# Softmax denominators as two products of 64 columns over 512 instead of four of 32 over 256

## The chip, the core and the metric

The kernel runs on one core of a Trainium2 chip. The metric is the device time of one execution in microseconds (us). The core has TensorE (PE in the profile; PEld is its weight load), VectorE (DVE), ScalarE (ACT), GpSimd (POOL), and a queue, SP, that issues all transfers.

## The reference

One transformer block in float32 on x of shape (2, 2048, 256): layer norm without weights, attention with 16 heads of 64 and a causal mask, an output projection, a residual sum, then layer norm, one linear layer (its weight is W plus a low-rank product) and a second residual sum.

```
qkv = layernorm(x) @ W_qkv                    # 256 -> 3 * 16 * 64
score = einsum('bihd,bjhd->bijh', q, k) / 8   # causal mask
wmat = softmax(score, axis=2)                 # over the keys j
x = x + einsum('bijh,bjhd->bihd', wmat, v).reshape(b, l, 1024) @ W_out
x = x + layernorm(x) @ (W + lilora_weight).T + b
```

The change is in the softmax: the sum over the keys, by which the product of the exponentials with v is divided.

## The kernel before

The program has three blocks, one behind the other: projection of q, k and v (`project_qkv`), attention (`attention`), and output projection with the linear layer (`project_and_ffn`). q, k, v and the attention's output `o_t` lie in DRAM between them.

Attention works on 16 items: 8 pairs of heads times 2 batches. The two heads of a pair share the 128 partitions, 64 each. An item has 4 tiles of 512 queries, t = 0 to 3. A unit (t, j) is 128 keys against the 512 queries of tile t, for both heads; tile t has 4(t + 1) units, so that an item has 40. All engines run an order written out by hand, over pairs of units:

- PE makes the scores of two units ahead (`score_unit`: float32r products of 64 rows and 128 columns, and small bf16 ones), chunks for the next item in between (`chunk_products`, L863: scores with queries as rows, of which DVE takes the row maxima), then the products with v for the two units (`pv_unit`, L899). The last are float32: weights of 128x64 for each head, the two heads side by side, over 512 columns of the exponentials. A float32 product shows as two matmul records, one for each of its two passes.
- ACT makes the exponentials (L964), copies the finished output of a tile out of PSUM (`copy_o`, L973), and at the start of an item also casts the next q and k.
- The exponentials `probs` are summed over the units, element by element: POOL adds the full units into `sum_pool` (L1147), DVE adds those on the diagonal and then `sum_pool` into `sum_dve` (L1059 to L1079). DVE also reduces the chunks to `part_max` (L1033).
- PSUM has a ring of three banks. A chunk takes two of them, a denominator one, in turn. PE waits before it reuses one, on DVE's reductions or on ACT's copy of the denominators (`ring_free`).

The denominators of tile t still need the sum of `sum_dve` over the 128 partitions. `denominators` makes it as a product with ones, which gives the sums to all rows of the output. It is queued on PE after the first pair of units of the next tile (for t = 3, of the next item). Then:

1. ACT copies the bank to `den_row` (L993), behind the exponential of the fourth unit of that tile.
2. SP sends one row of each product to `den_spread` (L742, `invert`), 4 values to a partition.
3. DVE takes the reciprocal (L1099), in its fixed order behind work of the sixth unit, so DVE stands still if the transfer has not landed.
4. SP stores it to `r_t` (L746), and loads it back with each head's row spread over 64 partitions (`recip`, two issues, L750).
5. POOL multiplies (`normalise`, `o_norm`, L1132), and SP stores the tile (L735).

SP runs all this in one order for an item: the last tile of the item before, then t = 0; the first half of a coming item's k and q (two loads of 512 KB, `load_piece`), t = 1; the second half, t = 2; at the end it places the row maxima of the next item in `shift` (`place_max`, four issues, L771). The first scores of the next item wait for these. Each `invert` comes behind the store of the tile before. The last item has no chunks. In it SP loads parts of `o_t` for the next block in these places.

The last denominators of all (item 15, t = 3) are made in the next block, in a bank of `y`, after the first tile of the output projection (L1368, L1407, `finish_last_o`).

Of the kernel before, what the change touches and what calls it, by code (L numbers as in the profile page):

```python
# [18 lines left out]
P = 128  # L19
# [8 lines left out]
TILE = 512  # L28
NB = TILE // P
EPS = 1e-5  # L30
STAGES = 3
DEN = TILE // 2
LOADS = 2
PARTS = 4
LOWEST = -3.0e38
# [27 lines left out]
def wait_apart(eng, sem, value, other, least):  # L63


    value = value if isinstance(value, int) else eng.to_reg(value)
    eng.wait_ge(other, least)
    eng.wait_ge(sem, value)
# [472 lines left out]
def attention(nc, q_t, k_t, v, o_t, r_t, w_out, batches, scale, consts, lead, tail):  # L541
# [5 lines left out]
    D = hd // HEADS  # L547
    assert 2 * D == P and batches == 2
    PAIRS = HEADS // 2
    TI = L // TILE  # L550
# [45 lines left out]
    ring_banks, at = {}, 0  # L596
# [58 lines left out]
    head = lambda h: slice(h * D, (h + 1) * D)  # L655
# [4 lines left out]
    with ctx:  # L660
        sb = lambda name, shape, dt=F32: ctx.enter_context(nc.sbuf_tensor("b_" + name, shape, dt))
# [11 lines left out]
        o_raw, o_norm, recip, sum_dve = tail["o_raw"], tail["o_norm"], tail["recip"], tail["sum_dve"]  # L673
        den_row, den_spread, recip_spread = tail["den_row"], tail["den_spread"], tail["recip_spread"]
# [8 lines left out]
        ring = ps("ring", [P, RING, TILE])  # L683
# [15 lines left out]
        den_copied, den_moved, inverted = tail["den_copied"], tail["den_moved"], tail["inverted"]  # L699
# [15 lines left out]
        with nc.Block() as block:  # L715

            @block.sync
            def _(sp):
# [18 lines left out]
                def invert(n, t):  # L737

                    wait_apart(sp, den_copied, n * TI + t + 2, o_stored, 1)
                    for c in range(4):  # L740
                        h, half = divmod(c, 2)
                        sp.dma_start(den_spread[half * D:(half + 1) * D, h, :], den_row[c * P // 4:c * P // 4 + 1, :].rearrange(  # L742
                            "o (p i) -> o p i", i=NB)).then_inc(den_moved, 16)

                    wait_apart(sp, inverted, n * TI + t + 1, o_stored, 1)
                    sp.dma_start(r_t[t].rearrange("h (p i) -> p h i", i=NB), recip_spread[:]).then_inc(inverse_stored, 16)  # L746

                    wait_apart(sp, inverse_stored, (n * TI + t + 1) * 16, o_stored, 1)
                    for h in range(2):
                        sp.dma_start(recip[h * D:(h + 1) * D, :], r_t[t, h:h + 1, :].broadcast_to([D, TILE])  # L750
                                     ).then_inc(recip_loaded, 16)
# [62 lines left out]
            def _(pe):  # L814
# [88 lines left out]
                def denominators(n, t, now, before):  # L903

                    pe.wait_ge(dve_added, sum_ready[n, t])
                    ring_free(now, before)
                    denom = ring[:, ring_banks["denom", t][0], :]
                    for c in range(4):
                        h, half = divmod(c, 2)
                        cols = slice(half * DEN, (half + 1) * DEN)  # L910
                        last = nc.tensor.matmul(denom[c * P // 4:(c + 1) * P // 4, 0:DEN], consts["ones"][:, 0:P // 4],
                                                sum_dve[t % 2][:, h, cols], start=True, stop=True)
                    last.then_inc(denom_made, 1)

                def item(pair, u, following, previous=True):
# [28 lines left out]
            def _(act):  # L944
# [43 lines left out]
                def copy_denominators(n, t):  # L988

                    act.wait_ge(denom_made, n * TI + t + 1)  # L990
                    act.wait_ge(den_moved, (n * TI + t) * 64 + 1)
                    denom = ring[:, ring_banks["denom", t][0], 0:DEN]
                    nc.scalar.copy(den_row[:], denom).then_inc(den_copied, 1)  # L993

                def item(pair, u, following, previous=True):
# [30 lines left out]
            def _(dve):  # L1026
# [68 lines left out]

                def reciprocals(n, t):

                    dve.wait_ge(den_moved, (n * TI + t + 1) * 64 + 1)
                    nc.vector.reciprocal(recip_spread[:], den_spread[:]).then_inc(inverted, 1)  # L1099

                def item(pair, u, following, previous=True):
# [59 lines left out]
def project_and_ffn(nc, x, o_t, r_t, bias, ffn_weights, out, consts, tail):  # L1161
# [10 lines left out]
    with ctx:  # L1172
        sb = lambda name, shape, dt=F32: ctx.enter_context(nc.sbuf_tensor("c_" + name, shape, dt))
# [27 lines left out]
        y = [ctx.enter_context(nc.psum_tensor(f"c_y{u}", [P, NB, cin], F32)) for u in range(2)]  # L1201
# [30 lines left out]
        all_pairs = HEADS // 2  # L1232
        o_tiles = tiles * all_pairs
        last_t = tiles // 2 - 1
        last_denom = y[1][:, 0, 0:DEN]

        with nc.Block() as block:

            @block.sync
            def _(sp):  # L1240
# [29 lines left out]
                def finish_last_o():  # L1270

                    sp.wait_ge(tail["den_copied"], o_tiles + 1)
                    for c in range(4):
                        h, half = divmod(c, 2)
                        sp.dma_start(tail["den_spread"][half * P // 2:(half + 1) * P // 2, h, :],
                                     tail["den_row"][c * P // 4:c * P // 4 + 1, :].rearrange("o (p i) -> o p i", i=NB)
                                     ).then_inc(tail["den_moved"], 16)

                    sp.wait_ge(tail["inverted"], o_tiles)
                    sp.dma_start(r_t[last_t].rearrange("h (p i) -> p h i", i=NB), tail["recip_spread"][:]  # L1280
                                 ).then_inc(tail["inverse_stored"], 16)

                    sp.wait_ge(tail["inverse_stored"], o_tiles * 16)
                    for h in range(2):
                        sp.dma_start(tail["recip"][h * P // 2:(h + 1) * P // 2, :],
                                     r_t[last_t, h:h + 1, :].broadcast_to([P // 2, TILE])).then_inc(tail["recip_loaded"], 16)

                    sp.wait_ge(tail["o_ready"], o_tiles + 2)
                    sp.dma_start(o_t[hd - P:hd, tokens - TILE:tokens], tail["o_norm"][:]).then_inc(tail["o_stored"], 16)
# [26 lines left out]
            def _(pe):  # L1316
# [45 lines left out]
                out_project(0, 0, [0, 1, 2, 3])  # L1362

                pe.wait_ge(tail["dve_added"], tail["dve_ops"])
                for c in range(4):
                    h, half = divmod(c, 2)
                    cols = slice(half * DEN, (half + 1) * DEN)
                    last = nc.tensor.matmul(last_denom[c * P // 4:(c + 1) * P // 4, :], consts["ones"][:, 0:P // 4],  # L1368
                                            tail["sum_dve"][last_t % 2][:, h, cols], start=True, stop=True)
                last.then_inc(tail["denom_made"], 1)  # L1370
                pe.wait_ge(merge_loaded, 16 * 5)
                nc.tensor.matmul(d_ps, down[:], aux[:], start=True, stop=True).then_inc(d_made, 1)
# [3 lines left out]
                for c in range(C):  # L1376
                    last = nc.tensor.matmul(l_ps[:, c, :], t_sb[:, c * P:(c + 1) * P], up_aux[:], start=True, stop=True)
# [7 lines left out]
            @block.scalar  # L1385
            def _(act):
                def high(T, u, loads):

                    act.wait_ge(o_loaded[u], (loads - (u == 0)) * 16)
                    act.wait_ge(y_made, T + 1)  # L1390
                    nc.scalar.copy(o_hi[u][:], o_in[u][:]).then_inc(o_hi_ready, 1)

                def take_root(T, u):

                    act.wait_ge(var_ready, T + 1)
                    nc.scalar.activation(root[u][:], var_eps[u][:], ACT.Sqrt).then_inc(root_ready, 1)  # L1396

                def turn(T, u):

                    act.wait_ge(transposed, T + 1)  # L1400
                    nc.scalar.copy(xt[u][:], turned[:]).then_inc(xt_ready, 1)

                act.sem_inc(y_made, 2)
                high(1, 1, 1)
                act.wait_ge(tail["denom_made"], o_tiles)
                act.wait_ge(tail["den_moved"], (o_tiles - 1) * 64 + 1)
                nc.scalar.copy(tail["den_row"][:], last_denom).then_inc(tail["den_copied"], 1)  # L1407
                take_root(0, 0)
                for i in range(halfway - 1):
                    turn(i * 2, 0)  # L1410
                    high(i * 2 + 2, 0, i + 2)
                    take_root(i * 2 + 1, 1)
                    turn(i * 2 + 1, 1)
                    high(i * 2 + 3, 1, i + 2)
                    take_root(i * 2 + 2, 0)
                turn(tiles - 2, 0)
                take_root(tiles - 1, 1)
                turn(tiles - 1, 1)

            @block.vector  # L1420
            def _(dve):
# [51 lines left out]
                dve.wait_ge(merge_loaded, 16 * 5)  # L1473
                nc.vector.tensor_tensor(w_ffn_t[:], l_ps, w_in[:], ALU.add).then_inc(merged, 1)
                norm(0, 0, 1)
                dve.wait_ge(tail["den_moved"], o_tiles * 64 + 1)
                nc.vector.reciprocal(tail["recip_spread"][:], tail["den_spread"][:]).then_inc(tail["inverted"], 1)
                for i in range(halfway - 1):
                    low(i * 2 + 2, 0)
# [31 lines left out]
def attend(nc, rows, w_qkv, w_out, bias, ffn_weights, out_rows, drams, batches, length, scale, consts):  # L1511
    q_t, k_t, v, o_t, r_t = drams
    with ExitStack() as ctx:
        sb = lambda name, shape, dt=F32: ctx.enter_context(nc.sbuf_tensor("f_" + name, shape, dt))
# [19 lines left out]
        with ExitStack() as later:  # L1534
            sb = lambda name, shape, dt=F32: later.enter_context(nc.sbuf_tensor("g_" + name, shape, dt))
# [5 lines left out]
                "o_norm": sb("o_norm", [P, TILE]),  # L1541
                "sum_dve": [sb(f"sum_dve{i}", [P, 2, TILE]) for i in range(2)],
                "recip": sb("recip", [P, TILE]),
                "den_row": sb("den_row", [P, DEN]),
                "den_spread": sb("den_spread", [P, 2, NB]),
                "recip_spread": sb("recip_spread", [P, 2, NB]),
                "o_in": [lead["raw"][:].rearrange("p a b (c t) -> p (a b c) t", t=TILE), sb("o_in1", [P, KC, TILE])],
# [69 lines left out]
```

## Time and profile before

| | |
|---|---|
| median of 3 runs | 1877.65 us (1874.08 to 1879.98) |
| the profiled execution | 1877.58 us, span 1875.8 us |
| mean granted clock of TensorE | 0.992 |
| PE, DVE, POOL, ACT busy | 95%, 66%, 52%, 42% |
| attention block | from about 330 to 1725 us of the span |

The span runs from the first to the last instruction of the core; the device time has 1.8 us around it. An idle time is put down to what ended it. Matmuls are pipelined, so that starts are firmer than ends.

### The profile page before, as it was taken

Reading aid. Unit: us, or ns where it says so; the run is one execution under the profiler, and the core shown is the slowest. Engines: PE = TensorE matmul, PEld = TensorE weight load, DVE = VectorE, ACT = ScalarE, POOL = GpSimd, SP = SyncE. Lnnn points to the kernel's source line nnn. Section 1 sums busy time; section 2 is a strip of 40 time slices with the busy share of each in tenths; the row PEclk is TensorE's granted clock in tenths of the full one; section 3 lists DMA queues with packets and bytes.
Section 4 is the critical chain, followed back from the end, with each engine's and each line's share of the span. In section 5 each row is a group of like instructions: output and inputs, shape, how many; then the busy total and the mean of one; then the engine's idle time right before and its main releaser. Section 6 shows DMA issues by size and latency. Waiting matters only on the chain. (4 is left out here: it accounts for less than half of the span.)

```text
span 1875.8 us, 34882 instructions
## 1 busy us (share of the span) xinstructions
PE 1780.3 (95%) x13720; PEld 1055.6 (56%) x13720; DVE 1246.0 (66%) x2091; ACT 789.0 (42%) x982; POOL 968.6 (52%) x532
## 2 busy tenths in 40 slices
PE   7999998999999999999999999999999999998998
PEld 5877776545545444445445455454554455444897
DVE  5364652767676767676767767676767677747565
ACT  3222113454545454545354454545454545454221
POOL 1011000666675758485766656676657585746211
PEclk9999999999999999999999999999999999999999
DMA  5646445212121212122121223121212121023551
GB/s 207 225 180 233 165 157 210 73 47 80 42 74 47 69 52 69 47 69 75 46 69 47 81 57 80 35 80 41 74 47 71 50 69 52 24 75 115 183 181 57
DMA packets 153858, 171.39 MB, mean 91 GB/s; under 512 B 48202, under 2 KB 94816, under 8 KB 153696
## 3 DMA queue, kind: packets, MB, share of 16 engines
q1 hardware_dynamic: 153696, 169.17, 28.7%
q8 instruction: 110, 1.80, 0.4%
q14 instruction: 52, 0.43, 0.1%
HBM read 97.02 MB, written 71.57 MB: 90 GB/s over the span
## 5 line engine op out<-in xcount | busy, mean ns | idle before, releaser
L1033 DVE TENSOR_REDUCE f_part_max<-b_ring 128x1 f32<-128x512 f32 (+3 forms) x1200 | 675.4, 604 | 290.5 <-PE b_ring L863 193.4
L964 ACT ACTIVATE b_probs<-b_scores 128x1024 f32<-128x1024 f32 (+3 forms) x640 | 564.6, 898 | 608.2 <-PE b_scores L834 342.7
L1147 POOL TENSOR_TENSOR b_sum_pool<-b_sum_pool,b_probs 128x1024 f32<-128x1024 f32 x237 | 569.4, 2403 | 32.1 <-POOL b_sum_pool L1147 0.5
L834 PE MATMUL b_scores<-b_split 64*128 64x512 f32 (+2 forms) x1920 | 296.8, 418 | 0.0
L834 PE MATMUL b_scores<-f_split 64*128 64x512 f32 (+2 forms) x1920 | 296.1, 416 | 0.0
L1147 POOL TENSOR_TENSOR b_sum_pool<-b_probs 128x1024 f32<-128x1024 f32 x48 | 114.7, 2389 | 309.8 <-DVE g_sum_dve L1079 198.1
L899 PE MATMUL b_o_acc<-b_probs,b_v_in 128*64 128x512 f32 (+3 forms) x1280 | 269.5, 542 | 2.3 <-ACT b_probs L964 2.3
L899 PE MATMUL b_o_acc<-b_probs,f_v_in 128*64 128x512 f32 (+3 forms) x1280 | 270.4, 543 | 0.0
L834 PEld LDWEIGHTS b_scores<-b_split 64*128 64x128 f32 x1920 | 179.8, 189 | 12.2
L834 PEld LDWEIGHTS b_scores<-f_split 64*128 64x128 f32 x1920 | 179.9, 188 | 11.0
L1073 DVE TENSOR_TENSOR g_sum_dve<-g_sum_dve,b_probs 128x768 f32<-128x768 f32 (+2 forms) x195 | 160.3, 822 | 35.5 <-ACT b_probs L964 30.9
L863 PE MATMUL b_ring<-b_split 64*128 64x512 f32 (+2 forms) x640 | 143.0, 434 | 18.3 <-DVE f_part_max L1033 17.3
L348 DVE COPY a_stage_d<-a_made 128x512 f32<-128x512 f32 x96 | 66.2, 691 | 140.8 <-PE a_made L293 140.7
L348 ACT COPY a_stage_a<-a_made 128x512 f32<-128x512 f32 x96 | 56.5, 589 | 224.7 <-PE a_made L293 223.4
L863 PE MATMUL b_ring<-f_split 64*128 64x512 f32 (+2 forms) x560 | 125.4, 436 | 17.4 <-DVE f_part_max L1033 16.3
L899 PEld LDWEIGHTS b_o_acc<-b_probs,b_v_in 128*64 128x64 f32 x1280 | 77.8, 136 | 112.2 <-issue 81.4
L899 PEld LDWEIGHTS b_o_acc<-b_probs,f_v_in 128*64 128x64 f32 x1280 | 77.9, 136 | 108.7 <-issue 80.9
L863 PEld LDWEIGHTS b_ring<-b_split 64*128 64x128 f32 x640 | 64.7, 183 | 128.6 <-issue 124.2
L830 PE MATMUL b_scores<-f_shift,p_first_rows 64*128 64x512 bf16 (+2 forms) x640 | 117.6, 356 | 14.8 <-ACT b_probs L964 10.5
L830 PE MATMUL b_scores<-b_shift,p_first_rows 64*128 64x512 bf16 (+2 forms) x640 | 118.2, 359 | 9.0 <-issue 4.6
L863 PEld LDWEIGHTS b_ring<-f_split 64*128 64x128 f32 x560 | 56.6, 184 | 114.6 <-issue 110.4
L712 POOL TENSOR_TENSOR b_split<-f_raw,b_split 128x512 fp32r<-128x512 f32 x64 | 81.5, 1297 | 59.6 <-ACT b_split L950 59.6
(138 smaller groups left out, 2219.2 us busy)
## 6 DMA issues: line engine op xcount, KB each, us to landing
f_raw<-k_t SPq DMA_DIRECT2D x32, 512.0 KB, 4.7
f_raw<-q_t SPq DMA_DIRECT2D x32, 512.0 KB, 5.8
g_recip<-r_t SPq DMA_DIRECT2D x128, 128.0 KB, 3.0
o_t<-g_o_norm SPq DMA_DIRECT2D x64, 256.0 KB, 2.0
q_t<-a_stage_a SPq DMA_DIRECT2D x32, 256.0 KB, 2.3
q_t<-a_stage_d SPq DMA_DIRECT2D x32, 256.0 KB, 2.0
k_t<-a_stage_a SPq DMA_DIRECT2D x32, 256.0 KB, 2.0
k_t<-a_stage_d SPq DMA_DIRECT2D x32, 256.0 KB, 2.0
```

The costliest lines, as they stand in the source:

```text
L348: copy(stage[e][s][:], made[:, g % BANKS, :]).then_inc(emptied[e], 1)
L712: vec.tensor_tensor(lo[u][:, cols], raw[p][:, which, inner], halves(hi[u][:, cols]), ALU.subtract).then_inc(split_lo, 1)
L830: nc.tensor.matmul(scores[s % 2][:, h, lo:TILE], consts["first_rows"][head(h), :], shift[u][head(h), queries], start=True, stop=False)
L834: last = nc.tensor.matmul(scores[s % 2][:, h, lo:TILE], a[u][head(h), keys], b[u][head(h), queries], start=False, stop=(term == 2 and not ...
L863: last = nc.tensor.matmul(rowwise[h][:, 0:wide], q_hi[u][head(h), ib * P:(ib + 1) * P], k_hi[u][head(h), c * TILE:c * TILE + wide], start= ...
L899: last = nc.tensor.matmul(o_acc[head(h), off:], v_in[u][:, j, head(h)], probs[s % PR][:, h, off:], start=(j == 0), stop=(j == NB * t + NB ...
L964: nc.scalar.activation(probs[s % PR][:, :, off:], scores[s % 2][:, :, off:], ACT.Exp, scale=scale).then_inc(exp_done, 1)
L1033: nc.vector.tensor_reduce(part_max[:, h, ib, c:c + 1], rowwise[h][:, 0:width], AX.X, ALU.max).then_inc(chunk_reduced, 1)
L1073: nc.vector.tensor_tensor(sum_dve[t % 2][:, :, off:], sum_dve[t % 2][:, :, off:], probs[s % PR][:, :, off:], ALU.add).then_inc(dve_added, 1)
L1147: nc.gpsimd.tensor_tensor(sum_pool[:], first, probs[s % PR][:], ALU.add).then_inc(pool_added, 1)
```

## The change

The product with ones had four parts: head h and half of the queries, weights of 128x32, 256 columns, each to its own 32 rows of the bank. Now it has two, one for each head: weights of 128x64, 512 columns, each to its own 64 rows. The bank's row 0 then has all 512 denominators of the first head and row 64 those of the second. So ACT's copy takes 512 columns instead of 256, `den_row` doubles, and SP sends two rows of 512 values (128 pieces of 16 bytes) instead of four of 256 (64 pieces each). The waits on `den_moved` count 32 for a tile instead of 64. The last denominators, in the third block, change in the same way, and their part of `y` is two sub-tiles wide instead of one.

```diff
 def invert(n, t):
-    for c in range(4):
-        h, half = divmod(c, 2)
-        sp.dma_start(den_spread[half * D:(half + 1) * D, h, :], den_row[c * P // 4:c * P // 4 + 1, :].rearrange(
+    for h in range(2):
+        sp.dma_start(den_spread[:, h, :], den_row[h * D:h * D + 1, :].rearrange(
             "o (p i) -> o p i", i=NB)).then_inc(den_moved, 16)
 def denominators(n, t, now, before):
-    for c in range(4):
-        h, half = divmod(c, 2)
-        cols = slice(half * DEN, (half + 1) * DEN)
-        last = nc.tensor.matmul(denom[c * P // 4:(c + 1) * P // 4, 0:DEN], consts["ones"][:, 0:P // 4],
-                                sum_dve[t % 2][:, h, cols], start=True, stop=True)
+    for h in range(2):
+        last = nc.tensor.matmul(denom[head(h), :], consts["ones"][:, 0:D],
+                                sum_dve[t % 2][:, h, :], start=True, stop=True)
 def copy_denominators(n, t):
-    act.wait_ge(den_moved, (n * TI + t) * 64 + 1)
-    denom = ring[:, ring_banks["denom", t][0], 0:DEN]
+    act.wait_ge(den_moved, (n * TI + t) * 32 + 1)
+    denom = ring[:, ring_banks["denom", t][0], :]
     nc.scalar.copy(den_row[:], denom).then_inc(den_copied, 1)
 def reciprocals(n, t):
-    dve.wait_ge(den_moved, (n * TI + t + 1) * 64 + 1)
+    dve.wait_ge(den_moved, (n * TI + t + 1) * 32 + 1)
...
-                "den_row": sb("den_row", [P, DEN]),
+                "den_row": sb("den_row", [P, TILE]),
```

## Rows read from the trace of the kernel before

**Rows 1.** The page's busy times: us, share of the span, instructions.

```profile
PE 1780.3 (95%) x13720; PEld 1055.6 (56%) x13720; DVE 1246.0 (66%) x2091; ACT 789.0 (42%) x982; POOL 968.6 (52%) x532
```

**Rows 2.** Windows: length, busy PE, PEld, DVE, ACT, POOL, granted clock, DMA share, GB/s.

```profile
412.60:1647.70 1235.10, 1186.61 (x10096) 617.25 (x10094) 886.75 (x1486) 588.81 (x727) 814.12 (x419) 1.00 0.22 60
...
412.67:500.10 87.43, 84.80 (x723) 43.95 (x721) 63.30 (x107) 42.17 (x53) 57.62 (x30) 1.00 0.22 62
```

**Rows 3.** Waits from 412 to 1640 us: who for whom, us in total, times, longest.

```profile
PE b_ring L863 <- DVE f_part_max L1033: 32.5, 49, 1.8
...
DVE g_recip_spread L1099 <- DMA g_den_spread<-g_den_row: 19.3, 26, 2.0
...
PE b_scores L830 <- issue: 6.5, 13, 1.5
```

**Rows 4.** Timeline of PE, item 1 (start us, us); middle two rows from narrower windows.

```profile
436.63 1.94 PE L899 MATMUL b_o_acc<-b_probs,b_v_in 128*64 128x512 f32 x8
438.50 0.64 PE L911 MATMUL b_ring<-g_sum_dve,p_ones 128*32 128x256 f32 x8
439.07 0.50 PE L863 MATMUL b_ring<-f_split 64*128 64x512 f32 x2
...
437.11 1.03 PE L899 MATMUL b_o_acc<-b_probs,b_v_in 128*64 128x512 f32 x4
...
437.54 1.03 PE L899 MATMUL b_o_acc<-b_probs,b_v_in 128*64 128x512 f32 x4
...
442.24 1.94 PE L899 MATMUL b_o_acc<-b_probs,b_v_in 128*64 128x512 f32 x8
444.11 0.50 PE L863 MATMUL b_ring<-f_split 64*128 64x512 f32 x2
```

**Rows 5.** ACT: copies by source line (ns min/median/max), and its timeline after one.

```profile
L993 ACT COPY g_den_row<-b_ring x63: 372/373/375, 334.6 to 1695.9; 128x256 f32<-128x256 f32 x63
...
L973 ACT COPY g_o_raw<-b_o_acc x64: 582/587/602, 329.8 to 1720.9; 128x512 f32<-128x512 f32 x64
...
422.63 1.96 ACT L964 ACTIVATE b_probs<-b_scores 128x1024 f32<-128x1024 f32 x2 [1.03 <-PE b_scores L842]
```

**Rows 6.** SP: issues by source line (ns), and a row of its timeline.

```profile
L742 SPq DMA_DIRECT2D g_den_spread<-g_den_row x252: 474/589/1832, 335.0 to 1698.2; - x126
...
L746 SPq DMA_DIRECT2D r_t<-g_recip_spread x63: 365/376/379, 344.2 to 1704.5; - x63
...
427.74 2.40 SPq L742 DMA_DIRECT2D g_den_spread<-g_den_row  x4
```

**Rows 7.** Timeline of DVE: reciprocals at t = 0 (three items) and t = 1.

```profile
431.38 0.20 DVE L1099 RECIPROCAL g_recip_spread<-g_den_spread 128x8 f32<-128x8 f32 x1 [0.29 <-DMA g_den_spread<-g_den_row]
...
785.72 0.20 DVE L1099 RECIPROCAL g_recip_spread<-g_den_spread 128x8 f32<-128x8 f32 x1 [1.97 <-DMA g_den_spread<-g_den_row]
...
1579.23 0.20 DVE L1099 RECIPROCAL g_recip_spread<-g_den_spread 128x8 f32<-128x8 f32 x1 [0.28 <-DMA g_den_spread<-g_den_row]
...
449.26 0.20 DVE L1099 RECIPROCAL g_recip_spread<-g_den_spread 128x8 f32<-128x8 f32 x1 [0.83 <-DMA g_den_spread<-g_den_row]
```

**Rows 8.** Timeline of PE: the last chunk of t = 0 in items 0 and 1.

```profile
348.83 0.50 PE L863 MATMUL b_ring<-b_split 64*128 64x512 f32 x2 [0.35 <-DVE f_part_max L1033]
...
436.21 0.49 PE L863 MATMUL b_ring<-f_split 64*128 64x512 f32 x2 [0.65 <-DVE f_part_max L1033]
```

**Rows 9.** Timelines of POOL, SP and PE up to the start of item 2.

```profile
465.96 22.53 POOL L1147 TENSOR_TENSOR b_sum_pool<-b_sum_pool,b_probs 128x1024 f32<-128x1024 f32 x9
...
492.07 0.59 SPq L771 DMA_DIRECT2D f_shift<-f_max_low  x1
...
493.89 0.39 PE L830 MATMUL b_scores<-f_shift,p_first_rows 64*128 64x512 bf16 x2 [0.22 <-issue]
```

**Rows 10.** Timelines of PE and DVE in the last item.

```profile
1671.34 1.08 PE L911 MATMUL b_ring<-g_sum_dve,p_ones 128*32 128x256 f32 x8 [2.28 <-DVE g_sum_dve L1079]
...
1682.68 0.20 DVE L1099 RECIPROCAL g_recip_spread<-g_den_spread 128x8 f32<-128x8 f32 x1 [11.39 <-DMA g_den_spread<-g_den_row]
```

More of the change, by code:

```diff
@@ L31 @@
 STAGES = 3
-DEN = TILE // 2
 LOADS = 2
@@ L1234, in project_and_ffn @@
         last_t = tiles // 2 - 1
-        last_denom = y[1][:, 0, 0:DEN]
+        last_denom = y[1][:, 0:2, :].rearrange("p n c -> p (n c)")
         with nc.Block() as block:
@@ L1272, in finish_last_o @@
                     sp.wait_ge(tail["den_copied"], o_tiles + 1)
[L1273 to L1277, printed above, removed]
+                    for h in range(2):
+                        sp.dma_start(tail["den_spread"][:, h, :], tail["den_row"][h * P // 2:h * P // 2 + 1, :].rearrange(
+                            "o (p i) -> o p i", i=NB)).then_inc(tail["den_moved"], 16)
                     sp.wait_ge(tail["inverted"], o_tiles)
@@ L1364, in _ @@
                 pe.wait_ge(tail["dve_added"], tail["dve_ops"])
[L1365 to L1369, printed above, removed]
+                for h in range(2):
+                    half = slice(h * P // 2, (h + 1) * P // 2)
+                    last = nc.tensor.matmul(last_denom[half, :], consts["ones"][:, 0:P // 2],
+                                            tail["sum_dve"][last_t % 2][:, h, :], start=True, stop=True)
                 last.then_inc(tail["denom_made"], 1)
@@ L1405, in _ @@
                 act.wait_ge(tail["denom_made"], o_tiles)
-                act.wait_ge(tail["den_moved"], (o_tiles - 1) * 64 + 1)
+                act.wait_ge(tail["den_moved"], (o_tiles - 1) * 32 + 1)
                 nc.scalar.copy(tail["den_row"][:], last_denom).then_inc(tail["den_copied"], 1)
@@ L1475, in _ @@
                 norm(0, 0, 1)
-                dve.wait_ge(tail["den_moved"], o_tiles * 64 + 1)
+                dve.wait_ge(tail["den_moved"], o_tiles * 32 + 1)
                 nc.vector.reciprocal(tail["recip_spread"][:], tail["den_spread"][:]).then_inc(tail["inverted"], 1)
```

## The prediction

> **What bounds the kernel now.** I read the page first [rows 1]: PE is busy 95% of the span, the next engine, DVE, 66%, and the clock is granted nearly throughout. Busy time alone proves little for pipelined matmuls, so I looked at the stretches next [rows 2]. The even part of the attention block, 412.6 to 1647.7 us, is 66% of the span, has PE busy for 1186.6 of its 1235.1 us (96%), and runs at the full clock (1.00, which is 2.4 GHz). The waits of PE in it [rows 3] are short: 32.5 us in 49 waits for `part_max` reductions on DVE and 6.5 us in 13 waits at the start of an item; those left are smaller. Together that is 3% of 1228 us. So a PE cost inside the block reaches the end of the kernel unless a wait that something else sets lies behind it. I therefore price the change on PE first, and then ask, for each of the four places where denominators are made in an item, whether the next wait is set by PE itself or by a chain that does not notice PE.
>
> **The product on PE.** The denominators run side by side in four column groups. They show as eight matmul records, two passes of four, and hold PE from 438.50 to 439.07, 0.57 us [rows 4]; the other products with a chunk behind them look the same. The new form is not in the trace, but its shape is: the product with V is two side-by-side 128x64 products over 512 columns in the same type. Eight of its records (two units, four passes) take 436.63 to 438.50, 1.87 us. Inside, a pass follows its like after 0.43 (437.11 to 437.54), the first pass takes 0.48, which leaves 1.87 - 0.48 - 2 x 0.43 = 0.53 for the last, whether a 128x32 product follows (438.50) or a 64x128 one (442.24 to 444.11, also 1.87). So I read 0.10 as the price of a change of shape. Before, there is such a change on both sides of the denominators. After, they have V's shape, and the one ahead goes. The step from the last pass of V to the next chunk is 0.53 + 0.57 = 1.10 before, and 0.43 + 0.43 + 0.53 = 1.39 after: **+0.29 us** each. From below, nothing cheaper than V's own passes is to be expected, since the columns that stream double; if the 0.10 ahead stayed it would be +0.39, and if the first pass were V's 0.48 too, +0.44. I take 0.29, because the last V pass costs the same whatever waits stand in front of the instruction behind it.
>
> The Trainium skill, TensorEngine Tiling (Array Packing), section Key Properties, says that changing the tiling mode drains the engine, while another tile of the same mode does not; by that rule the increment is 0.29, without it 0.39. The same page's section When to Use Tiling gives 64 columns a factor of two where 32 have four, which speaks against the change; the records of V and of the denominators agree.
>
> **ACT.** The copy of 256 columns takes 0.373, one of 512 columns from PSUM 0.587 [rows 5]: +0.21 us, 64 times. After the copy ACT idles 1.03 us for scores [rows 5], which PE makes later by the same amount as it ends the product, so the copy hides with 0.8 to spare. At t = 3 (15 times) ACT has casts of the next item around it and that idle time isn't there; PE is two units of scores behind ACT then, and I take it as hidden too. Without that cover its price would be 0.21 x 15 = 3 us.
>
> **The DMA chain.** SP issues four pieces in 2.40 us, 0.6 each (427.74 to 430.14), and the reciprocal starts at 431.38 [rows 6, 7]. A store of 256 pieces of 16 bytes takes SP 0.37 [rows 6], so an issue doesn't grow with its pieces in this range; two issues save 2 x 0.62 = **1.24 us** of the chain. The bounds are 0 (an issue of 128 pieces costs twice one of 64) and 1.24.
>
> **Which place is worth what.** Item n holds tiles t = 0 to 3; the product for a tile comes after the first V pair of the next.
> - t = 3 (15 times): nothing external follows soon. +0.29 each, **+4.4**.
> - t = 0 (n = 0 to 14 here, 15 times): +0.29 each, +4.4. In items 1 to 14 SP can send these denominators only after it has issued the store of the previous tile's `o_norm`, and DVE stands idle at the reciprocal for them: 0.29 in the first of the 14, 1.97 in the worst, 0.28 in the last, 8.8 in sum [rows 7]. Behind the reciprocal on DVE are the reductions that free the ring for PE. PE waits 0.65 for them at 436.21, but only 0.35 at 348.83 in item 0, where the reciprocal had no wait [rows 8]; the 0.30 is the missing 0.29. So this idle passes to PE one for one. With 1.24 less chain and 0.29 more PE time ahead, all goes but 0.4 of the worst: **-8.4**.
> - t = 1 (15 times): +0.29 each, **+4.4**. DVE idles at this reciprocal too (0.83 at 449.26), behind two 512 KB loads that SP issues just ahead [rows 7], so earlier issues hardly move the landing. PE makes the chunks around it without a wait, since two of the ring's three banks are ahead of DVE there. No gain is booked.
> - t = 2 (15 times): absorbed. POOL adds for t = 3 without a gap, nine adds from 465.96 in 22.53 us, then makes `o_norm`; SP stores it, and only then issues the four pieces that place the next maxima, the last at 492.07. PE's first score of the next item waits for these, until 493.89 [rows 9]. Thirteen such waits are listed, 6.5 us, 0.5 on average, 0.22 in the case shown, from a modelled end of the matmul before [rows 3, 9]. The chain starts before the product of t = 2 and hears nothing of it, so a PE that comes 0.29 later waits 0.29 less: **0**. The shortest waits may leave 0.07 each, 1 us in all; uncovered it would be +4.4.
> - The last item (no chunks): PE waits 2.28 for DVE at 1671.34, which comes out of a wait for `den_spread`, and DVE waits 11.39 for the next one [rows 10]. The three products of this item are absorbed. These two landings are behind 512 KB loads again, so out of 2 x 1.24 I book half, **-1.2**.
> - Tail: one product more on PE in the first output tile, **+0.3**.
>
> Sum: 13.1 - 8.4 - 1.2 + 0.3 = **+3.8 us**. The profiled execution took 1877.58, span 1875.8 and 1.8 around it, and the median of the runs is 1877.65, so both give 1881.4; I say **1881**. That is 0.2%, and a measurement of this kernel can tell 0.3% (5.6 us) from no change.
>
> **Rivals.**
> 1. The change of shape costs nothing, and the 0.10 stays ahead of the product: 45 x 0.39 = 17.6, and 15 x 0.05 more where the item's start absorbs only about 0.34. 17.6 + 0.8 - 9.6 + 0.3 = +9, 1887. For it: before, a product of V never has another tile's product of its own shape behind it, only its own next unit. Against: the even 0.53.
> 2. The DMA relief does not come, as 128 pieces cost twice an issue or land later. Then at t = 0 DVE's idle only shrinks by the 0.29 that PE is late, 4.1 in 14: 13.1 - 4.1 + 0.3 = +9, 1887. Against it is the 0.37 row.
> 3. Nothing absorbs, PE alone sets the time: 64 x 0.29 = +19, 1896. Against it are the waits of rows 7 to 9.
> 4. Faster: the reciprocal's idle passes to PE at t = 1 as well. Its 26 waits between 412 and 1640 sum to 19.3 [rows 3], of which t = 0 holds 8.8; if all went, 13.1 + 0.3 - 19.3 - 1.2 = -7, 1870.5. It falls below the 0.3% from about 17.8 us of them. Against it are the loads ahead.
>
> Single issues of `den_spread` took up to 1.83 us where the median is 0.59 [rows 6]. Which items these hit will differ from run to run, 1.2 us each, and I allow plus or minus 3 us for it in any case.
>
> **The numbers.** Forecast 0.60 (its own range 1877 to 1886), rivals 1 and 2 0.13 and 0.12, rival 3 0.07, rival 4 0.08. Below -0.3%: 0.08. Beyond +0.3%: rival 3, nearly all of 1 and 2 (0.22), and 0.12 of the forecast, 0.41. The rest, 0.51, is within. The range reaches to rivals 1 and 2 with 3 us behind them, and halfway to rival 4: 1873 to 1890.
>
> **What would show it.** Right: half as many records of the product (four for each) in about 0.96 us to the next chunk, and a last V pass of 0.43 ahead of them; copy 0.59; two issues in 1.2; hardly any idle at the t = 0 reciprocals, PE's wait in that place near 0.35, and the start-of-item waits 0.3 shorter. Wrong: a product of 1.05 or more, `den_spread` landing as late as before, or items that grow by 1.2 us each (no absorption). An item here goes 87.43 us in its undisturbed form [rows 2]; I expect 88.0.

## The result

The changed kernel takes 1881.27 us (median of 9 runs, 1878.58 to 1885.05), the kernel before on the same chips 1876.92 (9 runs, 1872.52 to 1882.61): a ratio of 1.0028, 95% interval 1.0015 to 1.0042. It is slower by 5.3 us, give or take 2.5; the forecast was 3.8. The ratios given here and below are estimates over all runs with their intervals, so they differ a little from the quotient of the two medians (here 1.0023).

The page of the changed kernel, its busy times [as rows 1]:

```profile
PE 1796.2 (96%) x13464; PEld 1063.3 (57%) x13464; DVE 1234.1 (66%) x2091; ACT 803.7 (43%) x982; POOL 962.6 (51%) x532
```

PE has 256 records fewer (64 products by 4) and is busy 16 us longer. Windows, as in rows 2: the same stretch, and item 1.

```profile
412.60:1647.70 1235.10, 1200.05 (x9876) 624.92 (x9874) 880.40 (x1487) 602.89 (x729) 807.22 (x419) 1.00 0.21 60
413.46:501.26 87.80, 85.84 (x708) 44.52 (x706) 62.56 (x107) 43.14 (x53) 57.66 (x30) 1.00 0.22 62
```

Waits from 412 to 1640 us, as in rows 3. All three fell:

```profile
PE b_ring L861 <- DVE f_part_max L1029: 23.2, 46, 0.8
...
DVE g_recip_spread L1095 <- DMA g_den_spread<-g_den_row: 7.1, 10, 1.3
...
PE b_scores L828 <- issue: 2.7, 4, 1.0
```

Timeline of PE at t = 0 in item 1, as in rows 4 and 8:

```profile
437.06 0.49 PE L861 MATMUL b_ring<-f_split 64*128 64x512 f32 x2 [0.33 <-DVE f_part_max L1029]
437.49 1.94 PE L897 MATMUL b_o_acc<-b_probs,b_v_in 128*64 128x512 f32 x8
439.26 1.03 PE L907 MATMUL b_ring<-g_sum_dve,p_ones 128*64 128x512 f32 x4
440.22 0.50 PE L861 MATMUL b_ring<-f_split 64*128 64x512 f32 x2
```

The product lasts 440.22 - 439.26 = 0.96 us up to the next chunk, and V's eight records before it take 1.77 instead of 1.87: the 0.10 of the change of shape ahead of it has gone. That is +0.29 us, as forecast.

ACT's copy, SP's issues by source line, SP's timeline, and the reciprocal on DVE at t = 0 of item 1, as in rows 5 to 7:

```profile
L989 ACT COPY g_den_row<-b_ring x63: 586/587/589, 335.4 to 1697.6; 128x512 f32<-128x512 f32 x63
...
L740 SPq DMA_DIRECT2D g_den_spread<-g_den_row x126: 494/590/1259, 336.1 to 1698.8; - x126
...
428.90 1.15 SPq L740 DMA_DIRECT2D g_den_spread<-g_den_row  x2
...
432.17 0.19 DVE L1095 RECIPROCAL g_recip_spread<-g_den_spread 128x8 f32<-128x8 f32 x1
```

An issue of 128 pieces takes what one of 64 took (0.59). The reciprocal no longer waits, neither here nor at t = 0 of any of the items 1 to 14.

To see where time goes by place, I took from PE's timeline the start of each product L907 (before: L911) and the distance to the next one. "t=0" is the distance from the product of t = 0 to that of t = 1, and so on; sums over items 0 to 14 in us, and in brackets how many of the 15 distances at t = 1 are 28.0 us or more.

```
kernel                            t=0     t=1          t=2     t=3    all
before                           278.1   414.9  (5)   511.2   117.2   1321.4
changed                          268.0   421.0 (11)   510.9   121.6   1321.5
wide product, four issues        273.8   422.2 (11)   510.0   121.6   1327.6
two issues, old product          267.8   413.0  (4)   512.0   117.2   1310.0
```

The last two kernels are experiments 1 and 2. t = 2 and t = 3 are as forecast. t = 0 gained more than forecast, and t = 1 lost more. The two profiled executions are 1.0 us apart (1877.58 and 1878.58) where the medians are 4.3 apart, as the profiled execution is the fastest of the changed kernel's nine; so the sums of one execution, which differ by only 0.1 us in all, can't be laid against the 5.3 of the runs; I take each as good to some 3 us. The usual (smallest repeated) distance is firmer: t = 0 18.00 before, 17.66 after; t = 3 7.81 and 8.11.

What happens at t = 1 shows in item 2 of the changed kernel: DVE, POOL and PE.

```profile
545.14 2.10 DVE L1055 TENSOR_TENSOR g_sum_dve<-b_probs 128x1024 f32<-128x1024 f32 x1
547.16 0.47 DVE L1029 TENSOR_REDUCE f_part_max<-b_ring 128x1 f32<-128x128 f32 x2
...
544.89 1.27 POOL L1128 TENSOR_TENSOR g_o_norm<-g_o_raw,g_recip 128x512 f32<-128x512 f32 x1
...
547.59 0.39 PE L861 MATMUL b_ring<-b_split 64*128 64x256 f32 x2 [0.66 <-DVE f_part_max L1029]
```

And the same place in the kernel before:

```profile
544.69 1.22 DVE L1059 TENSOR_TENSOR g_sum_dve<-b_probs 128x1024 f32<-128x1024 f32 x1
...
544.71 2.33 POOL L1132 TENSOR_TENSOR g_o_norm<-g_o_raw,g_recip 128x512 f32<-128x512 f32 x1
```

Before, DVE's first add of tile 2 starts 0.02 us ahead of POOL's multiply; the add takes 1.22 and the multiply 2.33. After, the multiply is 0.25 ahead; it takes 1.27 and the add 2.10. The later of the two seems to stand still until the earlier is done: 544.89 + 1.27 + 1.22 is 547.38, the add ends at 547.24. Nearer than that the records don't tell who wins: in items 6 and 14 of the kernel before the multiply is recorded 0.01 us behind the add, and it is the add that takes 2.36. DVE's order follows PE, which is 0.29 later by the product at t = 1; POOL's multiply comes behind its own splits and does not notice. When DVE loses, its reduction comes late, and PE waits 0.66 for the ring. The Trainium skill, SBUF — State Buffer, section "SBUF: two separate sides", says so: GpSimd and a VectorE operation with two inputs in SBUF take a shared pair of ports by an exclusive lock, the first holds it for the whole instruction and the other blocks. The trace agrees, 2.10 and 2.33 in place of 1.22 and 1.27.

### The profile page after: what moved, and what is told of

It reads as the page before. It is cut to its first block and busy times, and to the rows that moved or that the text cites. A ratio compares the mean times of both kernels' runs of the same rounds, so it can differ in the third digit from the quotient of the medians.

```text
span 1876.8 us, 34242 instructions
## 1 busy us (share of the span) xinstructions
PE 1796.2 (96%) x13464; PEld 1063.3 (57%) x13464; DVE 1234.1 (66%) x2091; ACT 803.7 (43%) x982; POOL 962.6 (51%) x532
## 3 DMA queue, kind: packets, MB, share of 16 engines
q1 hardware_dynamic: 151648, 169.16, 28.2%
q8 instruction: 108, 1.77, 0.4%
## 5 line engine op out<-in xcount | busy, mean ns | idle before, releaser
L1069 DVE TENSOR_TENSOR g_sum_dve<-g_sum_dve,b_probs 128x768 f32<-128x768 f32 (+2 forms) x195 | 155.7, 798 | 37.0 <-ACT b_probs L960 32.5
```

Source lines behind the costliest of these rows:

```text
L1069: nc.vector.tensor_tensor(sum_dve[t % 2][:, :, off:], sum_dve[t % 2][:, :, off:], probs[s % PR][:, :, off:], ALU.add).then_inc(dve_added, 1)
```

## The experiments

Each ratio is against the kernel before on the same chip, with its 95% interval.

**1 and 2. The two halves of the change.** The wide product and copy with four issues of half rows, and the reverse.

```diff
-            den_row[h * D:h * D + 1, :]                                    # changed: two issues
+            den_row[h * D:h * D + 1, half * DEN:(half + 1) * DEN]          # 1: four issues
```
```diff
-    for c in range(4): ... dma_start(den_spread[half * D:(half + 1) * D, h, :], den_row[c * P // 4:c * P // 4 + 1, :]
+    for h in range(2): ... dma_start(den_spread[:, h, :], den_row[h * D:h * D + 1, :]   # 2: product and copy as before
```

> The change's products (2 x 64 columns over 512) and its copy of 512 columns, but four issues of 64 pieces as before. My theory: t = 3 to t = 0 grows by 0.29 us an item as in the change; t = 0 to t = 1 stays near its 18.00 us (the 0.29 goes into DVE's idle time at the reciprocal, which shrinks but doesn't vanish); t = 1 to t = 2 takes 27.57 or, where POOL's multiply starts ahead of DVE's first add, 28.2; together about +9 to +12 us on before, ratio 1.005 to 1.006. Rival (the two issues bring nothing): like the change itself, ratio 1.003, and t = 0 to t = 1 at 17.66 as in the change.

> The old products (4 x 32 columns over 256) and the old copy, but the change's two issues of 128 pieces from a row of 512 values. The second 256 values of each row are ones, so half of the queries are divided by 1: that part of the result is left out. My theory: DVE's idle time at the t = 0 reciprocal goes, t = 0 to t = 1 falls from 18.00 to 17.4 us (17.66 of the change less the 0.29 of its product), nothing else moves: -8 to -14 us, ratio 0.993 to 0.9955. Rival (the relief is worthless, the change's shorter t = 0 comes from somewhere else): ratio 1.000.

Measured: 1 took 1886.62 us, 1.0052 (1.0033 to 1.0071), or +9.8 us. 2 took 1870.95, 0.9970 (0.9958 to 0.9982), or -5.6 us. Together +4.2 beside the change's +5.3, so the parts add up. The relief is real (rival 2 falls) but smaller than the 8.4 and 1.2 booked. The distances at t = 0 usually are 17.95 us in 1 and 18.00 before, 17.66 in the changed kernel and 17.68 in 2: with four issues as with two, the product there costs nothing. At t = 1 long distances go with the wide product (11 in 1, 4 in 2), not with the issues.

**3. Wide product at t = 2 alone.**

```diff
-    for c in range(4): ...                 # four products of 32
+    if t == 2: ... # two products of 64 over 512, copy of 512
+    else: ...      # as before, and four issues everywhere
```

> Products and copy in the new form at t = 2 only, the old form elsewhere, four issues everywhere. My theory (the wait at the item's start absorbs it): t = 2 to t = 3 stays at its 33.87 us although the product's step is 0.29 longer, and the ratio is 1.000. Rival (PE's time passes to the end): t = 2 to t = 3 at 34.16, +4.4 us, ratio 1.0023.

Measured: 1877.03, 1.0003 (0.9991 to 1.0015). t = 2 is absorbed: its sum is 511.9 (511.2 before). The usual distance is 34.00 and not 33.87 as expected, because the stretch now starts some 0.10 earlier, with the change of shape ahead of its product gone, and still ends with one; the stretch ahead of it is 0.09 shorter (27.19 for 27.28).

**4. The change of shape.** The change with 32 columns of ones instead of 64, over 512.

```diff
-    nc.tensor.matmul(denom[head(h), :], consts["ones"][:, 0:D], ...)
+    nc.tensor.matmul(denom[h * D:h * D + P // 4, :], consts["ones"][:, 0:P // 4], ...)
```

> The change with its two products 32 columns wide instead of 64, still over 512: the same columns stream, but the shape differs from V's. My theory (a change of shape costs 0.10): the step from V's last pass to the next chunk is 1.48 us where the change has 1.38, the last V pass back at 0.52; 45 x 0.10 = +4.5 us on the change, ratio 1.005 to before. Rival (only streamed columns count): step 1.38, ratio as the change, 1.003.

Measured: 1887.65, 1.0057 (1.0038 to 1.0075). Its PE timeline:

```profile
438.40 1.94 PE L897 MATMUL b_o_acc<-b_probs,b_v_in 128*64 128x512 f32 x8
440.27 1.05 PE L907 MATMUL b_ring<-g_sum_dve,p_ones 128*32 128x512 f32 x4
441.25 0.49 PE L861 MATMUL b_ring<-f_split 64*128 64x512 f32 x2
```

V's records take 1.87 again, with the same columns streamed and the same transfers as the change, so the 0.10 hangs on the shape of what follows. The run is 5.4 us above the change where 4.5 was expected. The Trainium skill (TensorEngine Tiling (Array Packing), Key Properties) calls it a drain; this run puts 0.10 us on one.

**5 and 6. The multiply held until DVE's first add of tile 2,** in the changed kernel (5) and in the one before (6).

```diff
     pool.wait_ge(o_stored, (n * TI + t) * 16 + 1)
+    if t == 1:
+        pool.wait_ge(dve_added, freed[n, starts_of[2] + 2 * NB][1])
     nc.gpsimd.tensor_tensor(o_norm[:], o_raw[t % 2][:], recip[:], ALU.mult)
```

> The change, with one wait more: POOL's multiply for tile t = 1 waits until DVE has done its first add of tile 2 (L1055). My theory (the product's 0.29 us lets POOL's multiply start 0.25 ahead of that add, which then takes 2.1 instead of 1.22 us and holds up PE): all first adds of tile 2 at 1.22, t = 1 to t = 2 at 27.57 in nearly every item instead of 28.2 in 11 of 15, -6 us on the change, ratio 0.9995 to before. Rival (the 28.2 has another cause, or the collision moves to the next add at the same price): t = 1 to t = 2 stays at 28.2 in most items, ratio 1.003.

> The kernel before with the same wait of POOL's multiply at t = 1. My theory: its 5 slow stretches from t = 1 to t = 2 (28.0 to 28.2) come to 27.28 as the others, -4.6 us, ratio 0.9975; the 10 fast ones are not changed. Rival (the collision moves on to the next add, or the later multiply holds up the store behind it): 1.000 or above.

Measured: 5 took 1879.38, 1.0005 (0.9995 to 1.0016), a gain of 4.3 us on the change where 6 was expected; 6 took 1881.82, 1.0010 (0.9999 to 1.0022), a miss. DVE and POOL in item 2 of kernel 5 tell why:

```profile
544.65 1.22 DVE L1055 TENSOR_TENSOR g_sum_dve<-b_probs 128x1024 f32<-128x1024 f32 x1
545.78 0.48 DVE L1029 TENSOR_REDUCE f_part_max<-b_ring 128x1 f32<-128x128 f32 x2
546.18 1.94 DVE L1069 TENSOR_TENSOR g_sum_dve<-g_sum_dve,b_probs 128x768 f32<-128x768 f32 x1
...
546.03 1.28 POOL L1130 TENSOR_TENSOR g_o_norm<-g_o_raw,g_recip 128x512 f32<-128x512 f32 x1 [1.73 <-DVE g_sum_dve L1055]
```

The first add is free (1.22 or 1.23 in all 15), but the multiply now starts 0.15 us ahead of the second one, 1.94 instead of 0.94. The distance at t = 1 is 27.9 us in nearly all items, between the 27.56 of an undisturbed one and the 28.2 of a lost first add: some 0.34 for every item. In kernel 6 it is 27.60 against 27.28, so 15 x 0.32 = 4.8 us for 5 first adds saved at up to 0.9 each, hence no gain.

**7. Wide product at t = 1 alone,** with four issues, as experiment 3 with `t == 1`.

> Products and copy in the new form at t = 1 only, the old form elsewhere, four issues everywhere. My theory (all of the harm of the new product is here): t = 1 to t = 2 at 27.57 less the change of shape that moves into the stretch before it, and 28.2 in some 11 of 15 items where before has 4 or 5: +4.2 for the product and +4 to +5 for the collisions, ratio 1.0045. Rival (the price is PE's 0.29 alone): +4.4 us, ratio 1.0023, with as many stretches at 28.2 as before.

Measured: 1882.71, 1.0020 (1.0011 to 1.0030). The time is the rival's. The profile has the theory's signs: first adds of 1.6 us or more in 10 of 15 items (5 before), and a sum at t = 1 of 423.9, 9.0 more than before. That execution took 1888.01, 5.3 above the median of its kernel, so I don't size the price of this place by it. Between 3.8 (runs) and 9 (one profile) it stays open.

**8. Both forms:** the new one at t = 0 and 2, the old at t = 1 and 3, with the wait of experiment 6.

```diff
+    WIDE = (0, 2)
+    if t in WIDE: ... # two products, copy of 512, two issues
+    else: ...         # four, 256, four
```

> The new form (products, copy, two issues) at t = 0 and t = 2, where the runs so far show its product at no cost, the old form at t = 1 and t = 3, and POOL's multiply at t = 1 waiting as in the two runs above. My theory: t = 0 to 1 at 17.66, t = 1 to 2 at 27.28, t = 2 to 3 at 33.88, t = 3 to 0 at 7.83: -5 us of DMA relief and -4.6 of collisions, ratio 0.9950. Rival (the parts don't add, because DVE and POOL fall on each other elsewhere): ratio 0.9975 or above.

Measured: 1871.99, 0.9967 (0.9954 to 0.9979): faster than both kernels, less than expected by the meeting with the second add (27.50 usual at t = 1).

**9, 10 and 11. The multiply held until the third add of tile 2,** in the changed kernel (9), in experiment 8 (10) and in the kernel before (11). The wait of experiments 5, 6 and 8 is for two adds more:

```diff
-        pool.wait_ge(dve_added, freed[n, starts_of[2] + 2 * NB][1])
+        pool.wait_ge(dve_added, freed[n, starts_of[2] + 2 * NB][1] + 2)
```

> The change, with GpSimd's multiply of the tile before (L1128) held at t=1 until VectorE has made its third add of tile 2, so that it falls beside a reduce out of PSUM (1.27 us at that place) and beside no add. If what the product at t=1 sets off is the meeting of that multiply with an add in SBUF, both places are gone: the stretch from the product at t=1 to that at t=2 is 27.56 us in nearly all items (28.2 in 11 of 15 with the change, 27.89 in all with the multiply behind the first add), the adds of 1024 and 768 columns take 1.22 and 0.94 us, and against the kernel before the ratio is about 0.9995 (0.998 to 1.0005). Rival: the meeting is not what makes the stretches long, or the store that is now 3 us later costs as much: stretches of 27.9 or more and a ratio of 1.001 or above.

> New form (two products, two issues) at t=0 and t=2, old form at t=1 and t=3, and the multiply held until the third add of tile 2. Theory: with the multiply behind the first add this mixture took 0.9967, its stretches after the product at t=1 27.50; they go to about 27.18, 0.32 less in 15 items, 5 us in all: a ratio of about 0.9945 (0.993 to 0.996). Rival: no gain beside the other place: 0.9965 or above, stretches of 27.5.

> The kernel before, with the multiply held until the third add of tile 2 alone. Theory: meetings cost the kernel before too, but in 4 or 5 items only: the stretches are 27.28 in nearly all items (sum over 15 about 411 for 414.9), a ratio of 0.998 (0.997 to 0.9995). Rival: no gain, 1.000 or above, as with the multiply held until the first add (1.0010).

Measured: 9 took 1874.29, 0.9979 (0.9968 to 0.9991). 10 took 1866.24, 0.9933 (0.9916 to 0.9949), the fastest of all. 11 took 1874.40, 0.9975 (0.9964 to 0.9986). Item 2 of kernel 9, DVE, POOL and SP:

```profile
545.93 1.22 DVE L1055 TENSOR_TENSOR g_sum_dve<-b_probs 128x1024 f32<-128x1024 f32 x1
547.07 0.48 DVE L1029 TENSOR_REDUCE f_part_max<-b_ring 128x1 f32<-128x128 f32 x2
547.47 0.95 DVE L1069 TENSOR_TENSOR g_sum_dve<-g_sum_dve,b_probs 128x768 f32<-128x768 f32 x1
...
550.21 1.29 DVE L1029 TENSOR_REDUCE f_part_max<-b_ring 128x1 f32<-128x512 f32 x2 [0.53 <-PE b_ring L861]
...
549.85 1.28 POOL L1130 TENSOR_TENSOR g_o_norm<-g_o_raw,g_recip 128x512 f32<-128x512 f32 x1 [4.14 <-DVE g_sum_dve L1069]
...
551.20 0.33 SPq L734 DMA_DIRECT2D o_t<-g_o_norm  x1
```

Both adds have their usual time, and the multiply and the reduction out of PSUM, which overlap from 550.21 to 551.13, have theirs too (1.28 and 1.29). The store comes 22.8 us behind the product at t = 1 (528.39), in the changed kernel 18.6 (527.62 to 546.23, the last number from SP's timeline); nothing pays for these 4.2 us. The distances, with the usual one at t = 1:

```
kernel                            t=0     t=1   (usual)   t=2     t=3
5 changed, behind first add      269.9   418.9  (27.89)  510.5   121.6
9 changed, behind third          270.2   412.7  (27.51)  511.3   121.6
6 before, behind first add       280.4   415.7  (27.60)  510.5   117.1
11 before, behind third          278.7   409.9  (27.22)  511.1   117.2
10 both forms, behind third      272.1   407.7  (27.12)  512.2   115.6
```

So the meetings at t = 1 cost the kernel before 414.9 - 409.9 = 5.0 us and the changed one 421.0 - 412.7 = 8.3 in the profiles. In the runs it is 0.25% of 1877, 4.7 us, and 0.49%, 9.2 us; their difference, 4.5, has an interval of some 4 us to both sides. With these meetings gone from both, the change is worth 0.9979 / 0.9975 = 1.0004, give or take 0.0016, nothing that can be measured (9 and 11 ran on the same chip, and their medians are 0.1 us apart).

**12. The old form at t = 3 alone,** the rest as changed (`WIDE = (0, 1, 2)`, no added wait).

> The change, with the product, the copy and the four issues of before at t=3 alone. It prices the product at t=3 by itself: the stretch from the product at t=3 to the next goes from 8.11 to 8.14 us back to 7.81 to 7.86, 0.29 in each of 15 items, so 4.4 us less than the change: a ratio of 1.0005 (0.9995 to 1.0015) against the kernel before. Rival: the 0.29 is made up for elsewhere at t=3 (the idle ahead of the reciprocals at t=0 is gone anyway), and the ratio stays at the change's 1.0028.

Measured: 1877.81, 0.9996 (0.9987 to 1.0004), that is 1.0028 - 0.9996 = 0.32%, 6 us below the change, give or take 3, so that the expected 4.4 is within. The sum at t = 3 is 115.7 for 121.6, 0.39 less each and not 0.29, because the 0.10 of the change of shape now stands at the end of the stretch ahead of it: at t = 2 the usual distance is 33.97 for 33.89, and V's records ahead of the product take 1.65 us for 1.55. That is behind the wait at the item's start, so nothing absorbs it, and 0.39 - 0.10 = 0.29 is left.

## Why the prediction was right

Time, sign and size hold: 3.8 us forecast, 5.3 with an interval of 2.8 to 7.9 measured. The prices on PE and at t = 2 and t = 3 were right; at t = 0 and t = 1 a mechanism was missing, and that its two effects nearly cancel is luck. Point by point:

- **The product, +0.29.** Right, at both ends of the step: 1.10 became 1.39 (0.43 and 0.96). That the change of shape ahead goes is shown by experiment 4. Rival 1 falls.
- **The copy,** +0.21 and hidden: 0.587 as read; experiment 3 has it at no price, and at t = 3 the distances grew by the product's 0.29 and no more.
- **t = 3, +4.4.** Right: 121.6 - 117.2 = 4.4, and experiment 12 gives 6, give or take 3.
- **t = 2, 0.** Right: 510.9 for 511.2, experiment 3 at 1.0003, and the waits of PE at the start of an item fell from 6.5 us in 13 to 2.7 in 4.
- **t = 0, +4.4 - 8.4.** The idle at the reciprocal did go (19.3 us of waits over all places are 7.1, and rival 2 falls by experiment 2), though the chain is 1.0 us shorter and not 1.24: from the first issue to the last landing at t = 0 it takes 3.61 before and 2.61 after (medians of items 1 to 14). But the net of -4.0 was too small. The usual distance fell by 0.34, 5.1 in 15, and the sum by 10.1 (with the meetings at t = 1 gone from both kernels, 278.7 - 270.2 = 8.5). The term that is off is the product's: it was to cost 0.29, and it cost nothing (17.66 with it, 17.68 without). The traces show why. In 11 of the 15 items of experiment 2 DVE's first add of tile 1 stands behind POOL's split, and PE then waits for the reduction behind the add. Item 3 of experiment 2 (old product), then of the changed kernel:

```profile
604.02 1.28 POOL L713 TENSOR_TENSOR f_split<-f_raw,f_split 128x512 fp32r<-128x512 f32 x1
604.80 1.58 DVE L1060 TENSOR_TENSOR g_sum_dve<-b_probs 128x1024 f32<-128x1024 f32 x1
606.86 0.44 PE L864 MATMUL b_ring<-f_split 64*128 64x384 f32 x2 [0.31 <-DVE f_part_max L1034]
...
605.70 1.29 POOL L711 TENSOR_TENSOR f_split<-f_raw,f_split 128x512 fp32r<-128x512 f32 x1
606.77 1.30 DVE L1055 TENSOR_TENSOR g_sum_dve<-b_probs 128x1024 f32<-128x1024 f32 x1
608.55 0.44 PE L861 MATMUL b_ring<-f_split 64*128 64x384 f32 x2
```

  With the old product the add starts 0.50 us before the split's end (605.30) and takes 1.58; with the wide one PE and DVE come 0.29 later, the add starts 0.22 before the end (606.99) and takes 1.30, and PE's wait of 0.31 is gone. So the 0.29 is taken out of time that DVE stood anyway. Summed over the 15 items this wait of PE is 6.7 us before and 6.0 in experiment 2, but 3.2 in experiment 1 and 3.5 in the changed kernel. In item 0 no POOL operation lies beside the add (1.22 in all four), and there the product does cost 0.30: 17.26 with the old one, 17.56 with the wide one. No run moved POOL's split by itself, so this is read from the traces and not tested.
- **t = 1, +4.4.** The working ("PE makes the chunks around it without a wait") missed that DVE comes 0.29 later too and falls behind POOL's multiply. The sum grew by 6.1, of which 8.3 - 5.0 = 3.3 are more meetings; in the runs the difference is 9.2 - 4.7 = 4.5. The product's own 0.29 is there (27.51 usual for 27.22 with the meetings gone), so the term is right and a second one is missing. This is the step that failed, and it makes the change slower: without it the ratio is 1.0004.
- **The last item, -1.2.** From its product at t = 0 to the last one it takes 83.8 us for 83.2, and 84.2 in experiment 2, where only the issues changed: no relief is seen, though 0.6 us of one execution proves no loss either. The second reciprocal in it comes 5.51 us after the first issue (1678.78 to 1684.29), before 5.44 (1677.24 to 1682.68). One such pair says little; at t = 1 of items 1 to 14, also behind two 512 KB loads, the last piece lands 5.22 us after the first issue where it took 5.52 (medians), so that 0.3 of the 1.0 us is left there.
- **Tail, +0.3.** From the last product to the end it takes 137.2 us for 137.3: not seen, and too small for one execution. No run tried it by itself.

The second landing in the last item of the changed kernel:

```profile
1678.78 1.15 SPq L740 DMA_DIRECT2D g_den_spread<-g_den_row  x2
...
1684.29 0.20 DVE L1095 RECIPROCAL g_recip_spread<-g_den_spread 128x8 f32<-128x8 f32 x1 [12.21 <-DMA g_den_spread<-g_den_row]
```

So the total came out near by two errors of opposite sign, t = 0 by 1 to 6 us better and t = 1 by 2 to 4 worse, with the 1.2 us of the last item missing. Both come from the same cause, which the prediction did not have: a DVE add and a POOL operation that hold each other up. Rival 4's mechanism is not seen either: experiment 2, with the same product and fewer issues, has the 27.28 of the kernel before at t = 1. Rivals 3 (1896) and 4 (1870.5) are out by the total.

## What to carry to other kernels

When an edit makes one engine late by a few tenths, look in the trace for a DVE operation with two inputs in SBUF and a POOL operation that overlap or start within that time of each other: in these traces the one that starts first goes on and the other stands still. The delay can turn the order over and then costs more than itself (0.29 became 0.9 on DVE at t = 1), or it falls into time in which DVE stands anyway and costs nothing (t = 0). Here an order cured it: one wait that puts POOL's multiply beside DVE's work out of PSUM took 0.25% off the kernel before and 0.49% off the changed one, about as much as the whole change moved or more. A wait that only moved the multiply to the next add did not (experiments 5 and 6). And where one operation is made at several places, price it at each and use each form where it is best: experiment 10 has 0.67% less time than the kernel before.

## What was unexpected of the hardware

- A DVE add of 128x1024 takes 1.22 us alone and 2.10 beside a POOL multiply that started 0.25 earlier; the multiply takes 1.27 alone and 2.33 when it starts 0.02 after the add. A reduction out of PSUM is not slowed by it: one of 128x512 takes 0.68 to 0.69 in the changed kernel, with a POOL operation beside it or not (a pair of them 1.29).
- Which of the two wins is settled within some 0.03 us: recorded starts that close don't tell it (items 6 and 14 before; one item of experiment 2).
- A product of 128x32 or 128x64 over the same 512 columns takes PE the same time up to the next chunk (0.98 and 0.96); that the old form was cheap lay in its 256 columns alone.
- SP issues 128 pieces of 16 bytes as fast as 64 (0.59 each).
